# A graph network on one core: the count packs of layer 0 stored in three pieces, one per group, instead of whole

## What is computed

```python
x = _layernorm(x + _L0_gnn_ref(x, src, dst, edge_weight), axis=-1)
x = _layernorm(x + _L1_gnn_ref(x, src, dst, ...), axis=-1)     # GCN convolution and a mixture of experts
x = _layernorm(x + _L2_gnn_ref(x, src, dst), axis=-1)
x = _layernorm(x + _L3_gnn_ref(x, edge_index, ...), axis=-1)
```

```python
x_hyp_agg = weighted_midpoint_spmm(x_hyp, C, rows, cols, vals)
num = jax.ops.segment_sum(vals[:, None] * gx[cols], rows, num_segments=N_NODES)
den = jax.ops.segment_sum(vals * (gamma[:, 0] - 1.0)[cols], rows, num_segments=N_NODES)[:, None]
```

## Time and profile before

| | |
|---|---|
| median of 3 runs | 8317.99 us (8314.03 to 8325.55) |
| the profiled execution, its own time | 8319.56 us |
| its span, first to last instruction | 8317.9 us |
| POOL busy | 5494.2 us (66%) |
| PE busy | 5061.5 us (61%) |
| DVE busy | 3892.7 us (47%) |
| ACT busy | 1913.4 us (23%) |
| layer 0: first scatter starts, last one starts | 242.35 us, 3467.88 us |

### The profile page before, as it was taken

One profiled execution on the slowest core, in us unless ns is written; L12 is line 12 of the kernel. 1 busy time (PEld: TensorE's weight loads), 2 busy tenths in 40 slices (PEclk: granted clock), 3 DMA queues, 4 the chain that ended last, 5 costly groups with the idle time before them and its releaser, 6 DMA issues. The chain is left out here.

```text
span 8317.9 us, 134079 instructions
## 1 busy us (share of the span) xinstructions
PE 5061.5 (61%) x32092; PEld 3584.8 (43%) x32093; DVE 3892.7 (47%) x17797; ACT 1913.4 (23%) x5420; POOL 5494.2 (66%) x4518
## 2 busy tenths in 40 slices
PE   0566565565666656337758746911875874775885
PEld 0455454454544444214434445810443542443444
DVE  2766666566666656452232364325323325223324
ACT  1233333333334434231101001302110112000103
POOL 0677777777777767547757754166775774775773
PEclk5777878888888878669979967955997996997998
DMA  9566666666666666776644403723442543442542
GB/s 197 62 60 62 64 65 66 70 74 79 76 80 85 87 84 92 136 199 188 190 132 161 136 33 103 206 58 107 149 150 97 169 157 116 150 152 97 169 157 83
DMA packets 1061261, 956.18 MB, mean 115 GB/s; under 512 B 249108, under 2 KB 960379, under 8 KB 1060882
## 3 DMA queue, kind: packets, MB, share of 16 engines
q0 software_dynamic: 316896, 288.98, 23.1%
q1 hardware_dynamic: 386052, 491.25, 19.9%
q10 hardware_dynamic: 357934, 171.68, 10.8%
HBM read 606.42 MB, written 327.65 MB: 112 GB/s over the span
## 5 line engine op out<-in xcount | busy, mean ns | idle before, releaser
L760 POOL DMA_INDIRECT sums<-work,idx x1564 | 2476.6, 1583 | 987.7 <-issue 391.0
L727 POOL DMA_INDIRECT work<-table,src_t x2385 | 2438.4, 1022 | 940.3 <-issue 713.4
L1249 PE MATMUL pp<-shared 128*128 128x378 bf16 (+8 forms) x8820 | 1920.6, 372 | 528.2 <-DMA shared<-counts 220.0
L1249 PEld LDWEIGHTS pp<-shared 128*128 128x128 bf16 x8820 | 897.3, 102 | 1362.0 <-issue 558.4
L1233 PE MATMUL pp<-work 128*128 128x128 f32 x4770 | 739.5, 303 | 755.2 <-DMA work<-table,src_t 558.8
L1666 DVE TENSOR_TENSOR acc<-acc,pp 128x128 f32 x597 | 172.2, 288 | 2017.3 <-PE pp L1233 2015.9
L1233 PEld LDWEIGHTS pp<-work 128*128 128x128 f32 x4770 | 654.2, 208 | 945.5 <-DMA work<-table,src_t 717.6
L1149 PE MATMUL pp<-acc 128*128 128x130 f32 x3128 | 560.0, 334 | 513.8 <-ACT work L913 509.7
L977 ACT ACTIVATE shared<-shared 128x128 bf16<-128x128 f32 x588 | 180.5, 307 | 2424.6 <-DVE shared L1673 1591.6
L1149 PEld LDWEIGHTS pp<-acc 128*128 128x128 f32 x3128 | 490.0, 238 | 532.6 <-issue 532.5
L913 ACT ACTIVATE work<-pp 128x520 f32<-128x520 f32 x391 | 236.2, 604 | 1581.3 <-DMA sums<-work,idx 1559.7
(11 more groups left out here) (303 smaller groups left out, 7015.3 us busy)
## 6 DMA issues: line engine op xcount, KB each, us to landing
shared<-counts SPq DMA_DIRECT2D x84, 661.5 KB
work<-table,src_t POOLq DMA_INDIRECT x2385
shared<-counts SPq DMA_DIRECT2D x42, 882.0 KB
shared<-counts SPq DMA_DIRECT2D x42, 840.0 KB
shared<-counts SPq DMA_DIRECT2D x42, 798.0 KB
shared<-counts SPq DMA_DIRECT2D x42, 787.5 KB
shared<-counts SPq DMA_DIRECT2D x42, 756.0 KB
shared<-counts SPq DMA_DIRECT2D x42, 735.0 KB
```

The lines of the kernel that those rows point to most:

```text
L727: pool.indirect_dma_start(out=msg[:, i % SLOTS, k, :], out_offset=None, in_=table, in_offset=bass.IndirectOffsetOnAxis(ap=src_t[:, at:at + ...
L760: pool.indirect_dma_start(out=sums0[k], out_offset=bass.IndirectOffsetOnAxis(ap=picked, axis=0), in_=rows, in_offset=None, bounds_check=NP ...
L1249: i = pe.matmul(bank[c][:, 0:COLS[n]].rearrange("p (k w) -> p k w", w=PACK * w), x3[:, b % 2, h, part3, :], ring[:, q % RING, 0:TB * COLS[ ...
```

## The change

The store of a pack moves out of `keep_counts` into a new function, and is cut in three along the 14 blocks: blocks 0 to 4, 5 to 9 and 10 to 13. The pieces are issued in the three groups that follow the pack, each right after `keep_rows` of its group and ahead of that group's count slices. `packed` now counts three landings per pack. For the pieces at the beginning of a span, which belong to the span before, `spans` writes out the first turn of every span, where before it did so once for the whole program. The code is the same for POOL and SP, but for the number that SP waits for.

```diff
+PIECES = ((0, 5), (5, 10), (10, NB))
...
         def spans(eng, body):
 
-            for s in range(SLOTS):
-                body(s, s, 0, 0)
             for n in range(len(SPANS)):
-                with eng.Fori(max(1, T0[n]), T0[n + 1]) as turn:
+                for s in range(SLOTS):
+                    body(T0[n] * SLOTS + s, s, T0[n], n, n if s >= PACK else n - 1)
+                with eng.Fori(T0[n] + 1, T0[n + 1]) as turn:
                     for s in range(SLOTS):
-                        body(turn * SLOTS + s, s, turn, n)
+                        body(turn * SLOTS + s, s, turn, n, n)
             for g in range(NU, NG):
-                body(g, g % SLOTS, g // SLOTS, None)
+                s = g % SLOTS
+                body(g, s, g // SLOTS, None, len(SPANS) - 1 if g < NU + PACK else None)
...
                 if place == 0:
-                    after(act, packed[buf], 16 * turn)
+                    after(act, packed[buf], len(PIECES) * 16 * turn)
...
-                if place == PACK - 1:
-                    size = TB * PACK * w
-                    act.wait_ge(evicted, u * SLICES + (EVICTED0 + SLICES))
-                    act.dma_start(counts_of[n].rearrange("b p c -> p b c")[:, :, ds(turn * (2 * size) + (buf - 2 * T0[n]) * size, size)],
-                                  stage[:, buf, 0:PACK * NT * w].rearrange("p (b c) -> p b c", b=NB)).then_inc(packed[buf], 16)
-
-            def rows_by_source(g, s, turn, n):
+
+            def store_counts(u, s, turn, n):
+
+                buf, place = 1 - s // PACK, s % PACK
+                size, nth = TB * PACK * WIDTH[n], (turn - buf) * 2 + buf
+                b0, b1 = PIECES[place]
+                if place == 0:
+                    act.wait_ge(evicted, u * SLICES + EVICTED0)
+                act.dma_start(counts_of[n].rearrange("b p c -> p b c")[:, b0:b1, ds(nth * size - 2 * T0[n] * size, size)],
+                              stage[:, buf, 0:NB * size].rearrange("p (b c) -> p b c", b=NB)[:, b0:b1, :]).then_inc(packed[buf], 16)
+
+            def rows_by_source(g, s, turn, n, stored):
...
                 keep_rows(s % 3).then_inc(rows_ready, 1)
+                if stored is not None and stored >= 0:
+                    store_counts(g, s, turn, stored)
                 if n is not None:
                     keep_counts(g, s, turn, n)
```

More of the change, by code:

```diff
@@ L356, in program @@
         CHUNK0 = [16 * KC * (NB // 2)] * 2 + [16 * (2 * TURNS + 1), 16 * 2 * TURNS]
-        r_in, ROWS0 = packed, 16 * DTURNS
+        r_in, ROWS0 = packed, len(PIECES) * 16 * DTURNS
         noted = sem("noted")
@@ L592, in _ @@
             for n in range(2):
-                sp.wait_ge(packed[n], 16 * DTURNS)
+                sp.wait_ge(packed[n], len(PIECES) * 16 * DTURNS)
             batches(sp, load_sums)
@@ L1189, in count_units, with products0 @@
                     i.then_inc(sliced, marks(n, j))
-            def products0(g, s, turn, n):
+            def products0(g, s, turn, n, stored):
                 next_of = lambda n: ((s + n) % SLOTS, turn + (s + n) // SLOTS)
@@ L1595, in unit_hots, with compare @@
                 i.then_inc(unit_hot, 1)
-            def compare(g, s, turn, n):
+            def compare(g, s, turn, n, stored):
                 if there(g + 1):
```

## The result

| | before | after |
|---|---|---|
| median | 8317.23 us (4 runs, 8314.03 to 8325.55) | 8027.88 us (4 runs, 8026.24 to 8028.62) |
| ratio | | 0.9656 [0.9644, 0.9668] |
| span of the profiled execution | 8317.9 us | 8026.1 us |

289 us less, against a forecast of 233 and a range that ended at 8040. The direction and the place were right, the size was not.

What follows compares the result with a forecast made beforehand. POOL's scatters were taken to bound layer 0, plus one store-caused stall per pack. Stalls of 258 us less 24 us left gave 234 us gain, 8319.6 - 234, stated as 8085 us; range 8040 to 8210, the forecast case's own 8038 to 8158.

Steps and rivals of the forecast that it cites:

- The bound: Layer 0: POOL's scatters set the pace, 7.43 us per group, plus one stall per pack from a store delaying a scatter.
- The stalls that can go: POOL's waits in layer 0 for landed scatters and ACT, beyond 0.30 us each: 258 us removed.
- I take the runs: A store's landing time goes by its number of runs, not bytes: 4.5 us per store beyond a fixed part.
- unexplained gaps: POOL's long gaps in layer 0 that the profile calls issue: 23 us, left in the forecast, gone only in its bound.
- 24 us of rest: Stalls left on POOL after the change: 10 us at width 19, 14 us allowed for the 360 other pieces.
- A piece of 5 of 14 blocks adds 5/14 of it: Slowest scatter beside a piece: delayed 2.1, 2.5 and 4.4 us at widths 6, 20 and 19; only width 19 late, 0.4 us.
- Hidden costs: ACT's 256 further issues, 97 us, covered by its waits for scatters; the wait for `packed` and written-out turns cost nothing.
- A (bytes): Stores on layer 0's scatters: delay goes by bytes, three pieces delay like one store; gain 24 us, 8296 us; chance 0.06.
- B: POOL's wait for scatters: any store delays equally however short, 0.98 us per piece, 377 us; slower, 8439 us; chance 0.06.
- C: Layer 0's packs: pieces of width 14 and more still hold up scatters; gain 122 us, 8197 us; chance 0.12.
- D: Engines ahead of POOL become the bound at widths 19 and 20: 24 us less gain, 8109 us; 0.74 together with the forecast.
- E: ACT's issue of stores: pieces come bunched instead of spreading over groups, giving no change; chance 0.02.

Runs made afterwards that it cites:

- the last runs: Four versions on one slower chip, ratios to the kernel before: the change 0.9504; its pieces behind the slices 0.952; with wider width-19 pitch 0.9501; two pieces, wider pitch 0.9518.

## Why the prediction was right in kind and too small

**The bound, right.** POOL's floor of 7.43 us per group and one stall per pack. Measured after: 2939.0 / 390.75 group lengths = 7.52 us, stalls gone.

One reading beside it was wrong. The prediction says that the scatter issued at 2396.47 holds up the one at 2404.50. Between the two lie three steps, not four, so they are not at the same place of their groups. The one at the same place is this; its landing stands below it:

```profile
2394.25 1.91 POOL L760 DMA_INDIRECT sums<-work,idx  x1 [0.30 <-issue]
```

```profile
DMA to landing us min/median/max: 9.4/9.4/9.4
```

POOL began it 0.40 us ahead of the store's issue, and it landed at 2403.6 us. So a scatter that starts just before a store is caught by it too.

**The stalls that can go, right:** 258 us, of which 257 went.

**"I take the runs", right in the main,** and shown by the thirds cut inside the runs: 811 us of stalls with the change's bytes and three times its runs. The argument from two rows of one view, 441 KB in 7.4 us and 1470 KB in 8.6, pointed the right way.

**What failed: how much was put down as left.** The steps are "Left: 24 pieces of width 19 at 0.4 us = 10 us, and for the 360 others I allow 0.04 us each = 14 us", and its lower bound, "nothing at all, with the 23 us of unexplained gaps going too, gives 281 us", which put the gain in longer scatters at nothing without a reason. Four terms of the sum were mis-sized:

1. 24 us of rest, measured 1.6. Of these, 10 were for width 19, from "A piece of 5 of 14 blocks adds 5/14 of it". This proportion failed at every width that can be compared: over the ordinary 3.4 us a piece adds 0.2 us to the slowest scatter at width 6, 1.4 at width 20 and 1.6 at width 19, where 2.1, 2.5 and 4.4 were forecast. A third of a store is much less than a third as harmful. The fixed 0.040 us per packet behind it did not hold either: it became 0.029. Why is not shown. On the chip of the last runs the change did have 8 us at width 19, but what the pieces add to a landing is not on record there. The other 14 us were a caution that no row supported; the margin of 1.5 us, which I had worked out myself, said zero.
2. 23 us of long gaps that the profile calls issue were counted as "unexplained" and left in. 17 of them went with the stalls, and 15 on the second chip, while 18 stayed where only the turns were written out. So a gap of 4.2 us where the ordinary one is 0.30 is most likely a stall whose releaser the profile could not name.
3. 48 us of longer scatters were taken as fixed, without a word. 12.5 went, for a reason that stays open.
4. 6.5 us beyond layer 0, within the spread of the runs before.

Together 22 + 17 + 12.5 + 6.5 - 1.2 = 57 us (the 1.2 us is by how much layer 0 began later), and 234 + 57 = 291 is the 292 us of span within a microsecond. **The range** ended at 281 us of gain, 8038 us, because it took only the waits and the issue gaps as what could go, and gave the overlength and the spread of the runs no room.

**Hidden costs, right.** ACT's 256 further issues (0.38 us, as forecast) show nowhere: ACT still waits 1323.1 us for scatters. `packed` holds nobody up: ACT's waits in layer 0 name scatters and PE, never a store. Writing out the turns: 1.0015.

**The rivals.** A (bytes) is refuted by the result and by the thirds of runs. B (the same delay however short the piece) failed for the change, yet comes near what happens when a piece keeps its 1792 runs (2.1 us each against 3.3 for a whole store). Of the two rules of the Trainium skill that were weighed, both on the page "DMA: Bandwidth & Descriptors", neither decided here. Coalescing (section "Rules for kernel authors") would have spoken for the slower whole store. The 2.0 us per DMA that the prediction gives with it stand in that page's section "Anatomy of one DMA", for DMAs that GpSimd issues; no run here shows them for ACT's stores. And taking turns packet by packet (section "Queues, rings and completion order") does not by itself explain a slowest scatter of 9.2 us beside a whole store and of 3.6 beside a third. C, D and E did not occur: no width kept its stalls, POOL's gaps put down to ACT fell to 1.2 us, and the pieces left one per group.

## What to carry to other kernels

- A store that nobody waits for can still be the costliest DMA of a loop. Look at what shares the DMA engines with the transfer that closes the loop's shortest cycle. Cut it so that each part lands inside the slack of one iteration, and put one part in each iteration; a cut that left the number of runs per part as it was made it worse here (ratio 1.0413).
- In the sum of a forecast, treat long gaps without a named releaser as part of the stall beside them, and let every excess over the floor (waits, unnamed gaps, longer instructions) bound the gain, not only the part with a name.

## What was not expected of the hardware

- With the same 1792 runs, 441 KB landed after 7.4 us and 1470 KB after 8.6. With the same bytes and three times the runs, stalls were 811 us, where the change had 2 to 11 us on three other chips.
- A third of a store added 0.2 us to the slowest scatter at width 6, where the whole store added 5.8.
- Rows 6384 bytes apart cost twice the stall of rows 6512 bytes apart, with the same runs: 6.2 against 3.0 us per store.
- Three DMAs back to back hold up scatters less than one with the same runs: 267 against 424 us.
- From chip to chip the same program took 8317 to 9063 us. POOL's floor was the same (7.42 to 7.45 us per group in the last groups of layer 0, in every profile). Two chips have profiles of the kernel before: the stalls of layer 0 are 54 us apart, and what makes up the rest, some 600 us in layers 1 to 3, is not shown.
